# Latent attention with one context product for two heads and values over four query tiles; other ends of two expert layers

## The reference

```python
def _L2_xattn_ref(x, latents, mask, ...):          # 8 heads of 64; x: context, 77 rows; latents: 512 rows
    kv_in = jnp.concatenate([xn, ln], axis=1)      # keys and values of 77 + 512 rows
    sim = jnp.einsum('bhid,bhjd->bhij', q, k)      # masked, then softmax over 589 keys
    out = jnp.einsum('bhij,bhjd->bhid', attn, v)
    return _ln(out @ w_out, g_o, b_o)

def _L1_ffn_ref(...):   # 8 experts, the best 2 of each of 2048 rows; experts of four kinds, 128 -> 512 -> 512 -> 128
    y = jnp.einsum('eth,te->th', out_e, w) + x

def _L3_ffn_ref(...):   # 8 experts, the best 2 of each row, and one shared expert for all rows
    shared_out = jnp.einsum('tsh,shd->td', jax.nn.silu(sg) * su, sw2)
    return (moe_out + shared_out).reshape(b, l, d)
```

## Time and profile before

| | us |
|---|---|
| median of 3 runs | 2335.51 (2330.65 to 2336.48) |
| profiled execution, its own time | 2335.52 |
| its span, first to last instruction | 2333.7 |
| first expert layer (l1f) | about 668 to 1080 |
| latent attention (l2x), loop of steps | about 1266 to 1610 |
| second expert layer (l3f) | about 2165 to the end |

### The profile page before, as it was taken

How to read it: one execution, slowest core, us unless ns; L and a number is a source line. 1 busy time by engine, 2 the same in 40 slices (tenths; PEclk the granted TensorE clock), 3 DMA queues, 4 the chain that set the end, 5 groups by cost and what they waited for, 6 DMA issues and landing times. The chain is left out here.

```text
span 2333.7 us, 35138 instructions
## 1 busy us (share of the span) xinstructions
PE 1852.5 (79%) x12537; PEld 1113.2 (48%) x12537; DVE 1495.2 (64%) x3419; ACT 1050.5 (45%) x2233; POOL 399.3 (17%) x576
## 2 busy tenths in 40 slices
PE   5768957999855999993777999996369999788862
PEld 3445542333353566651454666664235445344562
DVE  3436658888664555554344676776869999666524
ACT  2335535777612333331223655553247777455221
POOL 0110020000042544432001000001020000100274
PEclk8779978999967999995677999998679999899897
DMA  3000000000025888861000000000000000000374
GB/s 83 0 1 1 1 1 1 1 1 1 1 90 216 291 305 302 293 223 37 1 1 1 1 2 1 1 1 17 0 1 1 1 1 2 1 1 1 88 217 119
DMA packets 42797, 134.78 MB, mean 58 GB/s; under 512 B 7117, under 2 KB 22529, under 8 KB 37443
## 3 DMA queue, kind: packets, MB, share of 16 engines
q1 hardware_dynamic: 36587, 121.30, 14.8%
q0 software_dynamic: 4992, 10.23, 1.6%
q10 hardware_dynamic: 1048, 1.01, 0.1%
HBM read 123.42 MB, written 11.45 MB: 58 GB/s over the span
## 5 line engine op out<-in xcount | busy, mean ns | idle before, releaser
L153 POOL TENSOR_SCALAR rstd<-MV 128x2 f32<-128x2 f32 (+1 forms) x100 | 24.3, 243 | 1187.9 <-DVE MV L125 1181.3
L845 DVE TENSOR_REDUCE l1aM<-PS 128x2 f32<-128x1024 f32 x128 | 152.8, 1219 | 23.7 <-PE PS L601 21.7
L763 ACT ACTIVATE l1aE<-PS 128x512 f32<-128x512 f32 x256 | 140.8, 595 | 48.2 <-PE PS L630 46.7
L1575 PE MATMUL PS<-WB,H 128*128 128x512 f32 x312 | 142.3, 599 | 1.2 <-ACT H L1692 1.2
L763 ACT ACTIVATE l3aE<-PS 128x512 f32<-128x512 f32 (+3 forms) x256 | 102.5, 443 | 48.5 <-PE PS L634 45.8
L2478 DVE TENSOR_REDUCE M<-PS 128x1 f32<-128x589 f32 x128 | 92.4, 763 | 34.2 <-PE PS L2289 34.2
L845 DVE TENSOR_REDUCE l3aM<-PS 128x2 f32<-128x256 f32 (+3 forms) x128 | 101.2, 817 | 20.2 <-PE PS L603 19.1
L2387 ACT COPY PT<-PS 128x512 f32<-128x512 f32 x128 | 69.0, 590 | 89.9 <-PE PS L2300 89.6
L2393 ACT ACTIVATE E<-PS,M 128x589 f32<-128x589 f32 x128 | 95.8, 762 | 22.7 <-DVE M L2478 22.6
L1692 ACT ACTIVATE H<-PS,WB 128x128 f32<-128x128 f32 x156 | 44.5, 368 | 121.1 <-PE PS L1566 121.1
L873 DVE SCALAR_TENSOR_TENSOR l3aE<-l3aE,l3aLB 128x2048 f32<-128x2048 f32 (+1 forms) x64 | 94.8, 1482 | 2.6 <-ACT l3aE L763 2.6
(11 more groups left out here) (696 smaller groups left out, 4785.4 us busy)
## 6 DMA issues: line engine op xcount, KB each, us to landing
WB<-in_experts SPq DMA_DIRECT2D x39, 1798.0 KB
TB<-mixed_tails SPq DMA_DIRECT2D x39, 384.0 KB
WB<-in_experts SPq DMA_DIRECT2D x39, 384.0 KB, 4.1
WB<-mixed_out SPq DMA_DIRECT2D x8, 256.0 KB, 4.8
YB<-expert_out SPq DMA_DIRECT2D x8, 256.0 KB, 4.7
WB<-in_fold SPq DMA_DIRECT2D x1, 1676.0 KB, 7.1
cols_l2x_sb<-in_cols_l2x SPq DMA_DIRECT2D x1, 1154.0 KB, 10.3
mixed_tails<-in_tails SPq DMA_DIRECT2D x1, 1152.0 KB, 8.8
```

What stands on the lines that cost most here:

```text
L763: nc.scalar.activation(E[0:kn, home(m, kt) + j, q0:S], PS[0:kn, 4 + n % 2, q0:S], ACT.Exp, scale=SCALE).then_inc(exp_done, 1)
L845: v.tensor_reduce(M[:, m % 2, qt, 2 * hp:2 * hp + 2], PS[:, bank:bank + 2, 0:kc], AX, ALU.max, negate=True).then_inc(pair_free, 1)
L1575: mm(o, H1[:, i % 3, c * P:(c + 1) * P], mid_w(i, c), start=(c == 0), stop=False)
```

## The change

In latent attention the context scores of both heads become one product with 154 columns and one mask product. The values wait until the four query tiles of a pair are ready and are then multiplied as 5 key tiles x 2 heads with 512 columns; these ten products of pair n stand on four steps, 4n+5 (two key tiles) to 4n+8 (one each), and the last pair's all stand on the last step. `PT` grows to hold two pairs, ACT copies C once for a pair. The misc units W to Y move from steps 2-7 to 5-10 of a batch, L to U from 5-8 to 6-9.

In the first expert layer ACT makes `gd` (8 instructions, ahead of its copies with gain) and `rep` (16, after the exponentials) instead of POOL; POOL keeps the two memsets; PE counts the marks before the fold's products; the second one-hot matrix is made in halves, after `high`, and the list starts after the first half; `list_vector` comes before the flags. Of the 8 DMAs at the end four are issued by ACT.

In the second expert layer only the first sixteenth of the shared expert's work stays in the prologue; the rest stands between the tiles of the loop, one unit at each second tile up to tile 30, and the buffers `SG`, `EO` and the PSUM banks are single. The exponential of the weights moves from behind the loop to ahead of it. The DMAs at the end are split in the same way.

```diff
@@ spread_vector
-        step(v.tensor_tensor(self.at_row[:, :, :], self.iota_b[:, :].unsqueeze(1).broadcast_to([P, 2 * N, P]),
-                             self.row_b[:, :].unsqueeze(2).broadcast_to([P, 2 * N, P]), ALU.is_equal))
         step.eng.wait_ge(tiled, 1)
-        v.tensor_tensor(self.high[:, :, :], self.at_tile[:, :, :],
-                        self.ids_b[:, :].unsqueeze(2).broadcast_to([P, 2 * N, T]), ALU.mult).then_inc(spread, 1)
-        step.wait()
+        step(v.tensor_tensor(self.high[:, :, :], self.at_tile[:, :, :],
+                             self.ids_b[:, :].unsqueeze(2).broadcast_to([P, 2 * N, T]), ALU.mult))
+        for c in range(2):
+            own = slice(c * N, (c + 1) * N)
+            v.tensor_tensor(self.at_row[:, own, :], self.iota_b[:, :].unsqueeze(1).broadcast_to([P, N, P]),
+                            self.row_b[:, own].unsqueeze(2).broadcast_to([P, N, P]), ALU.is_equal).then_inc(spread, 1)
@@ list_tensor
         for m in range(last + 1):
+            if m % (BT * NT) == 0:
+                pe.wait_ge(spread, m // (BT * NT) + 1)
@@ experts_one, tensor
             route(3)
+            pe.wait_ge(marked, 1)
+            disp.count_tensor(COUNTS, counted)
             pe.wait_ge(centred, 2)
...
-            pe.wait_ge(marked, 1)
-            disp.count_tensor(COUNTS, counted)
-            pe.wait_ge(spread, 1)
             pe.wait_ge(lowered, 1)
@@ experts_one, gpsimd
-                if b == 0:
-                    pool.wait_ge(fold_in, 16)
-                    g.tensor_tensor(gd, fold["down"].rearrange("p (c d) -> p c d", c=8), fold["g1"].unsqueeze(2).broadcast_to([P, 8, P]),
-                                    ALU.mult).then_inc(scaled, 1)
-            for a, n in enumerate(("s1bb", "b1")):
-                g.tensor_tensor(rep[:, a], k.ones.unsqueeze(1).broadcast_to([P, 8, P]), fold[n].unsqueeze(2).broadcast_to([P, 8, P]),
-                                ALU.mult).then_inc(scaled, 1)
-            g.memset(TL[:, :, :], 0.0).then_inc(scaled, 1)
-            g.memset(RB[:, :, :], 0.0).then_inc(scaled, 1)
+            g.memset(TL[:, :, :], 0.0).then_inc(cleared, 1)
+            g.memset(RB[:, :, :], 0.0).then_inc(cleared, 1)
@@ experts_one, scalar
+            act.wait_ge(fold_in, 16)
+            for q in range(8):
+                ins = nc.scalar.mul(gd[:, q, :], fold["down"][:, q * P:(q + 1) * P], fold["g1"][:, q:q + 1])
+            ins.then_inc(scaled, 1)
...
-            act.wait_ge(scaled, 4)
+            for a, n in enumerate(("s1bb", "b1")):
+                for q in range(8):
+                    ins = nc.scalar.mul(rep[:, a, q, :], k.ones, fold[n][:, q:q + 1])
+            ins.then_inc(scaled, 1)
+            disp.spread_scalar(act, tiled, lowered)
+            act.wait_ge(cleared, 2)
@@ latent_attention, the order
-                late.setdefault(s0 + 2 + i, []).append((c, b - 1))
+                late.setdefault(s0 + 5 + i, []).append((c, b - 1))
...
-                late.setdefault(s0 + 5 + i, []).append(u)
+                late.setdefault(s0 + 6 + i, []).append(u)
...
+    values = {}
+    for n in range(NG // NT):
+        for i, ts in enumerate(((0, 1), (2,), (3,), (4,)) if n < NG // NT - 1 else (range(5),)):
+            values[NT * n + 5 + i] = (n, ts)
@@ latent_attention, tensor
-                    for par, c0 in enumerate((0, S - SC)):
-                        o = PS[:, at_ + 1, c0:c0 + SC]
-                        mm(o, Q[:, b % 2, pp, q], Kc[:, b % 2, pp, par, 0:SC], start=True, stop=False)
-                        mm(o, k.ones_b, k.kmask_b[:, b, 0:SC], start=False, stop=True)
+                    mm(context(s), Q[:, b % 2, pp, q], Kc[:, b % 2, pp, :, 0:SC], start=True, stop=False)
+                    mm(context(s), k.ones_b, k.kmask_b[:, b, 0:SC].unsqueeze(1).broadcast_to([P, 2, SC]), start=False, stop=True)
...
-                            ins = mm(PS[64 * par:64 * par + 64, 6, 0:P], Va[:, b % 2, t, h * DH:(h + 1) * DH],
-                                     PT[:, ring(j, par), t, :], start=(t == 0), stop=(t == len(KT) - 1),
-                                     skip_group_check=True)
+                            ins = mm(PS[64 * par:64 * par + 64, 6, :], Va[:, b % 2, t, h * DH:(h + 1) * DH], PT[:, n % 2, par, t, :],
+                                     start=(t == 0), stop=(t == len(KT) - 1), skip_group_check=True)
@@ experts_two
+    shared = [u for b in range(BT) for u in (("up", b, 0), ("up", b, 1), ("down", b, 0), ("down", b, 1))]
+    between = {2 * n: u for n, u in enumerate(shared)}
...
+                if i in between and i:
+                    what, b, c = between[i]
+                    (shared_up if what == "up" else shared_down)(b, c)
                 down(i)
```

More of the change, by code:

```diff
@@ L1713, in _ @@
                     take(i + 2)
+            act.wait_ge(o_taken, T)
+            for j in range(RING):
+                act.wait_ge(scattered[j], 16 * len(range(j, T, RING)))
+            for b in range(BT):
+                lo = B * S + b * S
+                act.dma_start(yb(1, b), placed[lo:lo + S, :].rearrange("(t p) d -> p t d", p=P)).then_inc(back[b], 16)
             for b in range(BT):
@@ new lines, in shared_down @@
+            def shared_down(b, half):
+                pe.wait_ge(eo_done, 2 * b + 2)
+                if half == 0:
+                    if b:
+                        pe.wait_ge(y_done, b)
+                    else:
+                        pe.wait_ge(known, 1)
+                for t in (2 * half, 2 * half + 1):
+                    for c in range(2):
+                        ins = mm(PS[:, 7, t * P:(t + 1) * P], EO[:, c, t * P:(t + 1) * P], w["w2"][:, c * P:(c + 1) * P],
+                                 start=(c == 0), stop=(c == 1))
+                ins.then_inc(d_ready, 1)
@@ L2753, in result, with share @@
                 v.tensor_copy(O[:, i % RING, :], PS[:, 4 + i % 2, 0:P]).then_inc(o_taken, 1)
+            def share(i):
+                what, b, c = between[i]
+                if what == "up":
+                    shared_hidden(b, c)
+                elif c == 1:
+                    shared_out(b)
             for i in range(T):
```

232 lines of the change are left out of this document (102 added, 130 removed).

## The result

The changed kernel took 2320.86 us (median of 5, 2319.07 to 2325.79), the one before beside it 2335.51 (2330.65 to 2337.86): ratio 0.9948, 95% interval 0.9929 to 0.9967. That is -14.7 us, where -27.8 was forecast: the direction held, about half of the gain is missing, and the time lies just above the range of 2298 to 2320.

What follows compares the result with a forecast made beforehand. PE was taken to set latent attention's pace, a prologue chain the first expert layer's changeable part, POOL the second's loop. From 2335.5, -10 - 11.5 - 6.3 = -27.8 gave 2307.7, say 2308; range 2298 to 2320.

Steps and rivals of the forecast that it cites:

- Latent attention, forecast -10: Latent attention: context scores, values, step places and end summed to -9.7, say -10 us, bounds -17 to +2.
- Where the gain counts: Latent attention: -12.6 in steps 5 to 64, -1.1 in 2 to 4, +1.9 DVE-paced, +3.1 end; moved misc units none.
- The longer `PT` adds no wait: Latent attention: the larger PT costs no wait, since its half is free two pairs earlier.
- First layer, -11.5: First expert layer: gathers 10.9 us earlier through the prologue, end -0.6; layer -11.5, bounds -13.5 and -6.
- Rival C: First expert layer: weights gate it, gathers early but tile 0 late, 4 to 5 us lost, 2312; within the forecast's 0.82.
- Second layer, -6.3: Second expert layer: gathers 4.3 us earlier, POOL's first-scatter wait at most 1.5 less, end -0.6; bounds -7.5 and +5.
- rival E: Second expert layer: the shared expert's work paces the last loop, +10 us, 2318; within the forecast's 0.82.
- The split reads: Ends of both expert layers: first pair of reads issued together, not one behind the other, -0.6 us each.
- B: Latent attention: DVE takes over as the bound, the step saves little and the stage gains 3, 2315; within the forecast's 0.82.
- A: Latent attention: long value products pay, a key tile costs 0.86, some 10 us more gain, 2298; chance 0.09.
- D: Latent attention: two heads' long value products not side by side, key tile 2.0 instead of 1.0, +80 us, 2388; chance 0.04.
- The rows above agree with the second: Latent attention values: rows side with the mode-change drain rule, not the cheaper long-product rule; values put at -1 us.

Runs made afterwards that it cites:

- pt_later: Changed kernel with POOL's memset of PT behind DVE's first norm instead of ahead of the first roots; ratio 0.9921 to the kernel before.
- heads_early: Changed kernel with L, M, T, U at steps 1 to 4 of a batch and PT cleared behind the first norm; ratio 0.9897 to the kernel before.
- l2x_only: Kernel before with the changed latent attention and nothing else of the change; ratio 1.0009 to the kernel before.
- after_again: Changed kernel unaltered, run once more with a second profile of its own; ratio 0.9934 to the kernel before.
- short_values: Changed kernel with values, PT, its memset and copies of C as before; 2313.53 us, ratio 0.9903 to the kernel before.
- context_only: Kernel before with one edit, both heads' context scores as one product and one mask; 2351.18 us against 2358.37, ratio 0.9973.
- warm: Changed kernel with ten short products, result unused, added in each of latent attention's steps 2 to 4; ratio 0.9956 to the kernel before.
- after: First profile of the changed kernel, unaltered, against the kernel before; median 2320.86 us, ratio 0.9948.
- ends_and_memsets: Changed kernel with all end reads by SP and the first expert layer's memsets behind DVE's last rows; ratio 0.9937 to the kernel before.
- shared_later: Changed kernel with the shared expert's units at tiles 8 to 36 of the last loop; ratio 0.9947 to the kernel before.

## Why the prediction was wrong, point by point

**Latent attention, forecast -10, came out +2.2.** The step that failed is "Where the gain counts" with the paragraph behind it. It counted what PE saves in each step and put at nothing what the change does to waits at the start and inside the loop: "may give 0 to 3 us; I take none" for the misc units that move, and "The longer `PT` adds no wait". The runs show +5.1 and +2.1 us in their place, and +3.4 by a clock that the sum took as constant. The prices were nearly right: context -0.17 to -0.18 a step (forecast -0.21), values -0.06 to -0.11 a pair (forecast -1 in all, that is -0.06), steps 3.84 and 4.70, end +3.4 (+3.1). What was missing:

| place | us | shown by |
|---|---|---|
| start: memset of PT ahead of the roots (+1.3); the rest (+0.8) goes with more of the start at 1.2 GHz | +2.1 | `pt_later` (both undone together) |
| steps 9, 25, 41: Q waits for ACT's copies of T and U, 8.18 against 6.05 - 0.41 + 0.86, 1.7 each | +5.1 | `heads_early` |
| steps 2, 3, 59 at 1.2 GHz: 4.6 (344.6 - 340.0 of `l2x_only`), less 1.2 at step 24 before | +3.4 | `after_again`, `l2x_only`; what moves the clock is open |
| end, against the forecast | +0.3 | rows above |
| rest, steps paced by DVE and by the norm of W to Y | +1.3 | difference, not shown |

-10 + 12.2 = +2.2. The first two are one mistake: I read an edit's waits for the buffers that it names and not for what it shares or feeds. The memset stands in POOL's queue ahead of the roots; T, whose copy Q reads, and U, whose bank Q takes over, moved to within a step of Q. I allowed the moved units a gain and no loss. Both could be read from the order and from rows of before. The clock could not: I took the 1.00 of the earlier trace rows for the stage after, which had 0.98 there.

**First layer, -11.5, came out -9.7** (-8.4 in the second profile). Stall on DVE stays, only earlier: yes, 8.35. Maxima 7.8 earlier (7.7), count wait 1.32 (1.0), gathers 11.0 earlier (10.9), first tile 11.1. Rival C did not come: at the first turn the wait is for rows, and in the loop PE waits nowhere over 0.5 us for weights. Missed: the ends (+0.4 for -0.6); the loop, which took 322.8 us from first tile to last scatter (323.5 in the second profile) where 321.8 stood, with its code unaltered and the cause not found; and again the clock: in `short_values` and `heads_early` the maxima came 3 us later (21.7 us into the layer against 18.6 to 19.1). Two windows of `short_values`, while PE works on the router, columns as in the earlier trace rows:

```profile
680.70:685.70 5.00, 5.00 (x25) 5.00 (x26) 4.86 (x16) 0.96 (x2) 2.01 (x1) 0.50 0.12 49
685.70:690.70 5.00, 5.00 (x26) 5.00 (x26) 0.83 (x2) 1.55 (x2) 0.00 (x0) 0.50 0.67 181
```

PE is busy without a pause at a granted clock of 0.50, 1.2 GHz, in the first of them; the same two stretches of the changed kernel's first profile had 0.71 and 0.63.

**Second layer, -6.3, came out -2.6 and -4.9.** Gathers -3.6 to -4.1 (-4.3), first scatter -5.0 to -5.4 (-5.8), both a little short. The likely reason is PE's clock: over the layer's first 40 us it was 0.54 and 0.60 in the two profiles, against 0.86 before, and the gathers came 0.5 us earlier in the one with 0.60. (The parts of this sum, 4.3, 1.5 and 0.6, add to 6.4, not 6.3.) The loop cost 2.0 in the first profile and 0.1 in the second: so rival E, the shared work as the loop's pace, did not come. The end +0.4 instead of -0.6.

**The split reads** were mis-signed: -0.6 each forecast, +0.3 and +0.4 found in the first pair of profiles. In the first layer all seven split profiles lie above all six with one queue; in the second layer the ranges overlap, so there only the missing gain is shown. I counted only the issue time of one queue; that the first pair then shares the DMA engines with six others is the likely reason, argued from the order of landing and not isolated. The Trainium skill (DMA: Bandwidth & Descriptors, Issuing engines are not separate DMA queues) says that issuing from several engines saves only the issue time; the trace agrees in that the split bought nothing but that, and in the first layer goes further, 0.1 to 0.5 us the other way.

**Rivals.** B (DVE takes over) fell: `context_only` has light steps of 4.07 with 0.17 gained. A fell: forty products of a pair became ten, and its time fell from 5.00 to 4.89. D fell: 1.01 for both heads' tile. The Trainium skill's figures in TensorE: Matmul & The Clock Gate, Back-to-back issue gap (81 ns for a product of 128 columns, 131 for one of 512) would by an estimate from them (131 against 4 x 81) have made the long form cost 0.4 of the short one; this case's trace has 0.98, for float32 products in half the array. The rule of TensorEngine Tiling (Array Packing), Key Properties (a change of mode drains the engine) is neither borne out nor refuted: no run here prices the switch alone, and "The rows above agree with the second" in the forecast says more than they show.

**What stays open.** The touched stages give -10.1 and -11.1 in the two profiles of after against the one of before, the medians -14.7 and -16.8 (2335.27 - 2318.43). The rest lies in stages with unaltered code, whose time varies by up to 8.7 us from build to build; what sets PE's clock in them was not tested.

## What to carry to other kernels

When an edit enlarges a buffer or moves a unit by one step, follow it down the queue of the engine that clears it, to the reader of what it makes and through the bank that it shares: the price of the operations was right to 0.04 us here, and the gain went into a memset ahead of a root and a copy ahead of a product. Undo one half of a combined change before keeping it: the context product alone shortened the stage by 4 us in spite of a slow step, the long values lengthened it by 3 to 9. A gain worked out from rows at 2.4 GHz needs a margin, since steps that the edit doesn't touch can come to lie at 1.2 GHz: 3.4 us in this stage.

## What the runs showed of the hardware

**One chip was slower in one stage only.** On the chip of `context_only`, `l2x_only`, `heads_early` and `warm` the kernel before takes 2358 us instead of 2335, and all of it lies in the last layer: 183.4 and 184.9 us with its code of before, against 161.8. ACT stands still there for some 3 us with its input ready, every four tiles or so, and DVE and PE behind it (`context_only`, ACT, DVE and PE; the scores of that tile were done at 2212.1):

```profile
2214.87 0.38 ACT L2682 ACTIVATE HG<-PS 128x256 f32<-128x256 f32 x1 [3.98 <-remote]
...
2215.28 0.42 DVE L2749 TENSOR_TENSOR HE<-PS,HG 128x256 f32<-128x256 f32 x1 [4.40 <-ACT HG L2682]
...
2215.76 0.71 PE L2633 MATMUL PS<-WB,HE 128*128 128x128 f32 x4 [3.64 <-DVE HE L2749]
```

The profile gives `remote` there, which is no instruction of this program; the cause stays open. Ratios from that chip are of the same program with a longer last stage; stage lengths of the attention agree with the other chips' (384.4 and 384.0).

**A memset on POOL holds some DVE instructions to its end, however small, and leaves others alone.** Held were casts and `tensor_scalar` from SBUF to SBUF: a cast of 128 x 64 took 3.19 us beside the memset of 3.57, 0.20 without; in the changed kernel a `tensor_scalar` of 128 x 128 took 3.68 us beside the memset of 3.73, 0.34 without. Not held, beside memsets of the same kernel: a `tensor_tensor` of 128 x 64 right ahead of that cast (0.23), the norms' statistics (0.28), and `tensor_scalar` out of PSUM (0.74 with and without). The Trainium skill (SBUF — State Buffer, Who interferes with whom) has the rule that a cast or `tensor_scalar` in a mode that takes the port pair shared with POOL is blocked for POOL's whole instruction, and that others are not beside one that only writes; the trace agrees. Moving the memset away from the rows moved the block to the casts.

**PE's clock repeats from run to run and is still not a property of the stage's code.** Four profiles (`after`, `after_again`, `ends_and_memsets`, `shared_later`) have steps 2 and 3 at 5.92 to 5.93 and 5.29 to 5.34 us, and `l2x_only` has 3.73 and 3.73 for the same code behind another program. Elsewhere it repeats less well: step 59 is 5.41 to 5.43 in three of the four and 4.75 in the fourth.
